# Masking the second attention's scores on TensorE, and handing its subtraction from GpSimd to VectorE

## What is computed

```python
q = (Q @ Wq_w + Wq_b).reshape(b, tq, H, DK).transpose(0, 2, 1, 3)      # 16 heads of 16
k = (K @ Wk_w + Wk_b).reshape(b, tk, H, DK).transpose(0, 2, 1, 3)      # 64 keys a batch
scores = jnp.einsum('bhqd,bhkd->bhqk', q, k) / jnp.sqrt(jnp.float32(DK))
scores = jnp.where(mask == 0, jnp.float32(-1000000000.0), scores)      # one mask of 512 x 64
attn = jax.nn.softmax(scores, axis=-1)
out = jnp.einsum('bhqk,bhkd->bhqd', attn, v)
x = x + jnp.tanh(g_xattn[1]) * (out @ Wo_w + Wo_b)
```

## Time and profile before

| | before |
|---|---|
| median of 3 runs | 811.75 us (811.11 to 812.29) |
| the profiled execution | 812.6 us, span 811.1 us |
| mean granted TensorE clock | 0.925 |
| busy in the span: PE, DVE, ACT, POOL | 82%, 63%, 41%, 28% |
| second attention's ticks, first `bounded` to the last tile's `bounded` | from 444.57 to 549.35 us |

### The profile page before, as it was taken

How to read it: one execution, slowest core, us unless ns; L and a number is a source line. 1 busy time by engine, 2 the same in 40 slices (tenths; PEclk the granted TensorE clock), 3 DMA queues, 4 the chain that set the end, 5 groups by cost and what they waited for, 6 DMA issues and landing times. The chain is left out here.

```text
span 811.1 us, 15016 instructions
## 1 busy us (share of the span) xinstructions
PE 666.6 (82%) x4947; PEld 613.2 (76%) x4948; DVE 510.2 (63%) x1271; ACT 328.9 (41%) x554; POOL 226.7 (28%) x336
## 2 busy tenths in 40 slices
PE   3798943898999889999734668686997889999995
PEld 3566633898999889998733446466997889999995
DVE  6844553788544786445577687794665775565556
ACT  7544313556333554334363354326432523343331
POOL 7532342000000000000064666367001711011152
PEclk9999855999999999999967789989998999999998
DMA  7999217544300359500040001000004411111124
GB/s 279 418 417 400 81 42 258 186 145 183 109 26 26 126 165 304 194 26 26 19 131 26 26 1 53 0 1 1 1 1 143 183 47 43 36 52 52 34 72 141
DMA packets 22997, 90.70 MB, mean 112 GB/s; under 512 B 4402, under 2 KB 8755, under 8 KB 17363
## 3 DMA queue, kind: packets, MB, share of 16 engines
q1 hardware_dynamic: 15794, 68.64, 22.9%
q0 software_dynamic: 7168, 21.63, 8.9%
HBM read 50.94 MB, written 45.61 MB: 119 GB/s over the span
## 5 line engine op out<-in xcount | busy, mean ns | idle before, releaser
L1559 ACT ACTIVATE e_h<-psum,e_be 128x256 f32<-128x256 f32 x144 | 67.6, 474 | 142.6 <-PE psum L52 140.1
L50 PE MATMUL psum<-e_h_hi,e_w_hi 128*128 128x256 f32 x384 | 110.3, 287 | 6.2 <-DVE e_w_lo L1631 5.5
L51 PE MATMUL psum<-e_h_lo,e_w_hi 128*128 128x256 f32 x384 | 107.9, 281 | 0.0
L52 PE MATMUL psum<-e_h_hi,e_w_lo 128*128 128x256 f32 x384 | 107.8, 281 | 0.0
L1623 DVE CAST e_h_hi<-e_h 128x256 fp32r<-128x256 f32 x144 | 43.5, 302 | 83.2 <-ACT e_h L1559 83.2
L1894 ACT ACTIVATE vz<-psum,fb 128x256 f32<-128x256 f32 x112 | 52.5, 475 | 99.9 <-PE psum L52 99.7
L50 PEld LDWEIGHTS psum<-e_h_hi,e_w_hi 128*128 128x128 f32 x384 | 72.3, 188 | 9.7 <-DVE e_w_lo L1631 8.8
L52 PEld LDWEIGHTS psum<-e_h_hi,e_w_lo 128*128 128x128 f32 x384 | 72.4, 188 | 0.0
L51 PEld LDWEIGHTS psum<-e_h_lo,e_w_hi 128*128 128x128 f32 x384 | 72.4, 188 | 0.0
L1625 DVE TENSOR_TENSOR e_h_lo<-e_h,e_h_hi 128x256 fp32r<-128x256 f32 x144 | 61.3, 425 | 4.9
L50 PE MATMUL psum<-e_gT_hi,e_w_hi 128*128 128x256 f32 x192 | 55.8, 291 | 9.5 <-DVE e_w_lo L1698 7.8
(11 more groups left out here) (415 smaller groups left out, 2144.2 us busy)
## 6 DMA issues: line engine op xcount, KB each, us to landing
xs<-zeros SPq DMA_DIRECT2D x18, 1024.0 KB, 17.6
e_w_raw<-in_W SPq DMA_DIRECT2D x18, 1024.0 KB, 5.2
ys<-zeros SPq DMA_DIRECT2D x6, 1024.0 KB, 24.1
ys<-e_yo POOLq DMA_DIRECT2D x14, 256.0 KB, 3.5
e_xg<-xs POOLq DMA_DIRECT2D x13, 256.0 KB, 6.5
e_w_raw<-in_W SPq DMA_DIRECT2D x6, 512.0 KB, 8.0
f_w_lo<-fw SPq DMA_DIRECT2D x6, 512.0 KB, 7.0
ys<-x_norm POOLq DMA_DIRECT2D x10, 256.0 KB, 2.5
```

The lines of the kernel that those rows point to most:

```text
L50: nc.tensor.matmul(out, wh, xh, start=start, stop=False)
L51: nc.tensor.matmul(out, wh, xl, start=False, stop=False)
L52: return nc.tensor.matmul(out, wl, xh, start=False, stop=stop)
L1559: nc.scalar.activation(h32[:, m % RING], ps[:, HIDDEN_BANKS[m % RING], 0:SLOT], ACT.Gelu, bias=be[:, m:m + 1]).then_inc(gelu_ok, 1)
```

## The change

A mask value is no longer applied by DVE as it reads the banks. `off` holds 0 or -2^100 for each row and key, in the form TensorE takes, and a fourth matmul for each bank (the identity times `off`, repeated for the 8 heads) adds it to the scores in PSUM. DVE then takes the maxima straight from the banks, and subtracts them from the banks again into `s_sc`; GpSimd's subtraction is gone. In its place GpSimd adds the two halves of each head's 64 exponentials into a tile `pairs` (16 x 32), which DVE sums. `scores(n+1)` waits for the end of DVE's subtraction, where it waited for the end of the clamping.

```diff
@@ gpsimd
             for n in range(NT + 1):
-                if n < NT:
-                    pool.wait_ge(mx_ok, n + 1)
-                    nc.gpsimd.tensor_tensor(sc[:, n % 3], sc[:, n % 3], top[:, n % 2, :, None].to_broadcast([P, HEADS, KEYS]),
-                                            ALU.subtract).then_inc(sub_ok, 1)
-                if 1 <= n < NT + 1:
+                if n:
+
+                    pool.wait_ge(p_ok, n)
+                    if n >= 2:
+                        pool.wait_ge(den_ok, n - 1)
+                    p = sc[:, (n - 1) % 3]
+                    nc.gpsimd.tensor_tensor(pairs[:], p[:, :, 0:KEYS // 2], p[:, :, KEYS // 2:KEYS], ALU.add).then_inc(add_ok, 1)
                     pool.wait_ge(sum_ok, n)
@@ vector
-            def bounded(n):
+            def differences(n):
+
                 dve.wait_ge(s_done, n + 1)
+                masked = ps[:, 6:8, :].rearrange("p c (h n) -> p (c h) n", h=HPC)
+                nc.vector.tensor_reduce(top[:, n % 2], masked, AX.X, ALU.max).then_inc(mx_ok, 1)
+                dve.wait_ge(mx_ok, n + 1)
                 if n >= 3:
                     dve.wait_ge(pt_done, n - 2)
-                nc.vector.scalar_tensor_tensor(out=sc[:, n % 3], in0=ps[:, 6:8, :].rearrange("p c (h n) -> p (c h) n", h=HPC), scalar=MASKED,
-                                               in1=cap[:, n % TB, None, :].to_broadcast([P, HEADS, KEYS]),
-                                               op0=ALU.max, op1=ALU.min).then_inc(cl_ok, 1)
-                dve.wait_ge(cl_ok, n + 1)
-                if n >= 2:
-                    dve.wait_ge(sub_ok, n - 1)
-                nc.vector.tensor_reduce(top[:, n % 2], sc[:, n % 3], AX.X, ALU.max).then_inc(mx_ok, 1)
+                nc.vector.tensor_tensor(sc[:, n % 3], masked, top[:, n % 2, :, None].to_broadcast([P, HEADS, KEYS]),
+                                        ALU.subtract).then_inc(sub_ok, 1)
 
             def reciprocals(n):
-                dve.wait_ge(p_ok, n + 1)
+                dve.wait_ge(add_ok, n + 1)
                 if n >= 2:
                     dve.wait_ge(nm_ok, n - 1)
-                nc.vector.tensor_reduce(den[:, n % 2], sc[:, n % 3], AX.X, ALU.add).then_inc(den_ok, 1)
+                nc.vector.tensor_reduce(den[:, n % 2], pairs[:], AX.X, ALU.add).then_inc(den_ok, 1)
@@ vector, constants
-            nc.vector.tensor_scalar(cap[:], mask_i[:], 0.0, HUGE - MASKED, ALU.not_equal, ALU.mult).then_inc(cap_ok, 1)
-            dve.wait_ge(cap_ok, 1)
-            nc.vector.tensor_scalar(cap[:], cap[:], MASKED, None, ALU.add).then_inc(cap_ok, 1)
+            nc.vector.tensor_copy(ident_r[:], k["ident"][:]).then_inc(off_ok, 1)
+            nc.vector.tensor_scalar(off[:], mask_i[:], 0.0, HIDE, ALU.is_equal, ALU.mult).then_inc(off_ok, 1)
@@ tensor
                 if n:
-                    pe.wait_ge(cl_ok, n)
+                    pe.wait_ge(sub_ok, n)
                 t = slice(i * P, (i + 1) * P)
                 for c in range(C):
-                    last = mm3(nc, ps[:, 6 + c, :], qT_hi[:, b % 2, c, t], qT_lo[:, b % 2, c, t],
-                               kz_hi[:, b, c, :], kz_lo[:, b, c, :], True, True)
+                    mm3(nc, ps[:, 6 + c, :], qT_hi[:, b % 2, c, t], qT_lo[:, b % 2, c, t],
+                        kz_hi[:, b, c, :], kz_lo[:, b, c, :], True, False)
+                    last = nc.tensor.matmul(ps[:, 6 + c, :].rearrange("p (h n) -> p h n", n=KEYS), ident_r[:],
+                                            off[:, i, None, :].to_broadcast([P, HPC, KEYS]), start=False, stop=True)
                 last.then_inc(s_done, 1)
```

More of the change, by code:

```diff
@@ L33 @@
 EPS = 1e-5
-MASKED = -1e9 * HD ** 0.5
 SCALE = HD ** -0.5
-HUGE = 3e38
+HIDE = -float(2 ** 100)
 RSQRT_SEED = 0x5F3759DF
@@ L711, in softmax_attention @@
         rw, rw_hi, rw_lo = sb("rw", [P, C, E1]), sb("rw_hi", [P, C, E1], F32R), sb("rw_lo", [P, C, E1], F32R)
-        mask_i, cap = sb("mask_i", [P, TB, KEYS], I32), sb("cap", [P, TB, KEYS])
+        mask_i, one = sb("mask_i", [P, TB, KEYS], I32), sb("one", [P, KEYS])
+        off, ident_r = sb("off", [P, TB, KEYS], F32R), sb("ident_r", [P, P], F32R)
+        pairs = sb("pairs", [P, HEADS, KEYS // 2])
         sc = sb("sc", [P, 3, HEADS, KEYS])
@@ L719, in softmax_attention @@
         uh_hi, uh_lo = (t[:].rearrange("p a c s -> p (a c s)").rearrange("p (m n) -> p m n", n=SLOT) for t in (qT_hi, qT_lo))
-        c_ld, cst_ok, cap_ok, bo0 = sem("c_ld"), sem("cst_ok"), sem("cap_ok"), sem("bo0")
+        c_ld, cst_ok, off_ok, bo0 = sem("c_ld"), sem("cst_ok"), sem("off_ok"), sem("bo0")
         wh_ok, wl_ok = sem("wh_ok"), sem("wl_ok")
@@ L728, in softmax_attention @@
         q_done, qh_ok, ql_ok = sem("q_done"), sem("qh_ok"), sem("ql_ok")
-        s_done, cl_ok, mx_ok, sub_ok, p_ok, den_ok, sum_ok, nm_ok = (
-            sem(n) for n in ("s_done", "cl_ok", "mx_ok", "sub_ok", "p_ok", "den_ok", "sum_ok", "nm_ok"))
+        s_done, mx_ok, sub_ok, p_ok, add_ok, den_ok, sum_ok, nm_ok = (
+            sem(n) for n in ("s_done", "mx_ok", "sub_ok", "p_ok", "add_ok", "den_ok", "sum_ok", "nm_ok"))
         pt_done, pc_ok, pv_done, oh_ok, ol_ok = (sem(n) for n in ("pt_done", "pc_ok", "pv_done", "oh_ok", "ol_ok"))
@@ L1029, in _ @@
             nc.vector.tensor_copy(bo_hi[:], bo[:]).then_inc(cst_ok, 1)
-            nc.vector.memset(cap[:, 0, :], 1.0).then_inc(cst_ok, 1)
+            nc.vector.memset(one[:], 1.0).then_inc(cst_ok, 1)
             dve.wait_ge(cst_ok, 3)
@@ L1033, in _ @@
             nc.vector.tensor_tensor(bo_lo[:], bo[:], f32(bo_hi[:]), ALU.subtract).then_inc(cst_ok, 1)
-            nc.vector.tensor_copy(ones_r[:].rearrange("p (a n) -> p a n", a=2), cap[:, 0:1, :].to_broadcast([P, 2, KEYS])).then_inc(cst_ok, 1)
-            dve.wait_ge(cst_ok, 6)
-            nc.vector.tensor_scalar(cap[:], mask_i[:], 0.0, HUGE - MASKED, ALU.not_equal, ALU.mult).then_inc(cap_ok, 1)
-            dve.wait_ge(cap_ok, 1)
-            nc.vector.tensor_scalar(cap[:], cap[:], MASKED, None, ALU.add).then_inc(cap_ok, 1)
+            nc.vector.tensor_copy(ones_r[:].rearrange("p (a n) -> p a n", a=2), one[:, None, :].to_broadcast([P, 2, KEYS])).then_inc(cst_ok, 1)
+            nc.vector.tensor_copy(ident_r[:], k["ident"][:]).then_inc(off_ok, 1)
+            nc.vector.tensor_scalar(off[:], mask_i[:], 0.0, HIDE, ALU.is_equal, ALU.mult).then_inc(off_ok, 1)
             norm_1(0)
@@ L1054, in _ @@
             norm_1(2)
-            dve.wait_ge(cap_ok, 2)
             for n in range(TICKS):
@@ L1058, in _ @@
                 if n < NT:
-                    bounded(n)
+                    differences(n)
                 if 1 <= n < NT + 1:
@@ L1178, in first_layer @@
                     if q < 2:
-                        pe.wait_ge(cl_ok, NT)
+                        pe.wait_ge(sub_ok, NT)
                     else:
@@ L1223, in _ @@
             pe.wait_ge(cst_ok, 6)
+            pe.wait_ge(off_ok, 2)
             pe.wait_ge(kzh_ok, HPC)
```

## The result

The changed kernel is slower: 827.24 us against 811.43 us for the kernel before on the same chip, a ratio of 1.0204 (95% interval 1.0174 to 1.0234). The profiled execution took 826.65 us, span 825.2 us, mean granted TensorE clock 0.923. The prediction was 825.3 us, 818.5 to 830.5.

The account below looks back on a forecast made before the run. The ticks were taken as bounded by waits between engines, mostly a chain of DVE, PE's scores, ACT's queue and DVE's sum. Nine terms summed to 13.6 us on the median 811.75, giving 825.3 us, range 818.5 to 830.5.

Parts of the forecast that it names:

- Banks free: Before the scores: banks held through maxima and then subtraction, so PE starts 1.25 us later wherever it waits for them.
- the items: The prediction's nine numbered terms along the chain of ticks 0 to 16, from -0.5 to +2.7 us, together 13.6 us.
- Two more matmuls: PE's scores: two more matmuls of 512 columns cost 0.47 us at full clock, 0.85 at half clock.
- Halving sum: GpSimd ahead of DVE's sum: 1.25 less 0.54, 0.7 us longer through exponential and sum; 0.54 shorter in DVE's queue alone.
- Item 3: Tick 4, where DVE's queue (a layer norm) sets the time: 0.5 us shorter.
- Behind 557.70 the shift is carried by a full PE: After tile 14's multiplication: GpSimd's last work at most 2 us later, hidden under PE work, so the shift stays 13.6 us.
- Item 8: Ticks 12 and 13: +0.7 us, GpSimd's long subtraction now standing before a sum that DVE waits for.
- DVE sets the period, and the time falls: Rival: the ticks' chain is DVE's queue, each of 16 ticks 0.54 us shorter, 803.1 us; 7 in 100.
- The milder one: Rival: the low end, around 820.5 us, as PE with more work in the scores may keep its clock; 25 in 100.
- The heavier one: Rival: around 829 us, from slow halving sums, half clock everywhere or a dearer PSUM read; 16 in 100.
- the 0.065 us: DVE's maxima: the skill page's estimate of a PSUM read's extra time over SBUF; the prediction left it out of its sum.

Follow-up runs that it names:

- pe_waits_max: Kernel before, with PE's scores waiting for the end of the maxima instead of the clamping: stretch 123.6 us, 8.9 more; ratio 1.0107.
- full_sum: Changed kernel without GpSimd's halving sum, DVE summing all 64 exponentials of a head: stretch 125.6 us, 7.6 less than the changed kernel; ratio 1.0110.
- exp_first: Kernel before, with ACT's exponential of the last tile only moved ahead of `q_hi` and the attention's high-half copy: stretch 111.5 us; ratio 0.9982.
- exp_early: Kernel before, exponential ahead of `q_hi` in ACT's queue and, every fourth tick, ahead of the transposes' copy: stretch 111.2 us, 3.6 less; ratio 0.9953.
- no_mask_mm: Changed kernel without the 32 matmuls that add the mask, so no mask is applied: stretch 132.3 us, 0.9 less; ratio 1.0171.
- late_w1: Changed kernel with GpSimd's second long weight subtraction moved from tick 15 to 16: stretch 131.0 us, 2.2 less; ratio 1.0198.
- extra_mm: Kernel before with the 32 mask matmuls added and DVE's clamping kept: stretch 120.1 us, 5.4 more; ratio 1.0051.
- halve_before: Kernel before with GpSimd's halving sum added behind its subtraction, DVE summing 32 instead of 64: stretch 143.3 us, 28.6 more; ratio 1.0349.
- after_early: Changed kernel with ACT's queue reordered as in exp_early: stretch 121.2 us; ratio 1.0075 to the kernel before.
- full_early: Changed kernel without its halving sum and with ACT's queue reordered as in exp_early: stretch 115.14 us; ratio 1.0023 to the kernel before.

## Why the prediction was right, and where it was not

**What held.** Sign, mechanism and size: 13.6 us forecast up to the multiplication of tile 14, 14.4 measured, and a median 2 us above the forecast one. The signs that it named came out: maxima and subtraction at 1.22, the halving sum at 1.27 (1.2 forecast), DVE's sum at 0.68, 116.3 us from the first to the last tile's reading (112 to 116 forecast). PE's wait for the banks rose to 19.7 us, just short of the "over 20" forecast. From `project(2)` to the first scatter of the routing it took 67.8 us instead of 67.2, so that part kept its length.

**Banks free (1.25 a pass).** Right in mechanism, shown alone by pe_waits_max: +8.9 us, where the items hold some 6.7 for it. The other 2.2 us go with the lower clock (0.79 instead of 0.86), which the items left to the matmuls' term; no run takes the two apart.

**Two more matmuls.** This term was mis-sized. The items hold some 3.6 us for it; the runs gave 0.9 (taken out of the changed kernel) and 5.4 (added to the one before). If the hold of the banks costs the changed kernel what it cost the one before, it is 2 us dearer than its items, and the matmuls, at 0.9, are 2.7 us cheaper: two errors of opposite sign, which the total hides. So the 0.8 us at the multiplication of tile 14 is in part luck.

**Halving sum.** 3.4 us in the items up to tile 14, 3.6 by full_sum. Item 3 was -1.1 instead of -0.5: the DVE instruction that reads two operands in SBUF took 1.74 us before (from 475.29 on, beside the end of GpSimd's subtraction, with GpSimd's multiplication from 475.90 on, itself slowed to 2.88 us), and 1.19 after. Timelines of the profile before and of the profile after:

```profile
475.29 1.74 DVE L948 SCALAR_TENSOR_TENSOR x_res<-x_norm,tg,x_res 128x1024 f32<-128x1024 f32 x1
```

```profile
474.04 1.91 POOL L810 TENSOR_TENSOR s_sc<-s_sc,s_top 128x1024 f32<-128x1024 f32 x1 [3.13 <-DVE s_top L978]
475.90 2.88 POOL L814 TENSOR_TENSOR s_sc<-s_sc,s_rden 128x1024 f32<-128x1024 f32 x1
```

```profile
474.39 1.19 DVE L951 SCALAR_TENSOR_TENSOR x_res<-x_norm,tg,x_res 128x1024 f32<-128x1024 f32 x1
474.56 2.79 POOL L817 TENSOR_TENSOR s_sc<-s_sc,s_rden 128x1024 f32<-128x1024 f32 x1 [2.28 <-DVE s_rden L988]
```

The Trainium skill, page "GPSIMD Engine Reference", section "Specifications", says that GpSimd and VectorE share their way to SBUF and get in one another's way when VectorE has two inputs there; the slowed pair of before agrees. After, only GpSimd's side of the pair is slowed. In these rows it is each time the instruction that started second that is longer: DVE's, 1.25 us into the subtraction, then GpSimd's multiplication behind it; after, GpSimd's, 0.17 us behind DVE's. Two places are too few for a rule.

**The step that failed** is "Behind 557.70 the shift is carried by a full PE: the last multiplication and the weights' subtractions on GpSimd come later by 2 us more at most, under several us of PE work". PE was not yet full: `project(2)` waits for an `xT_lo` that stands in DVE's queue behind the last sum, and that sum now waits for GpSimd. Item 8 had found this very link behind tick 12; behind tick 15 I followed the multiplication and not DVE's queue. It cost 4.0 us, shown from two sides: gone without the halving sum, and 2.2 us smaller with the long subtraction moved. That the median is off by only 2 us although this is missing is in part luck: the profiled execution of the changed kernel started the stretch 2.8 us early. On the second chip the change cost 17.4 us of the median (817.62 to 835.0), nearer to the stretch's 18.4 than to the 13.6 forecast.

**The rivals.** *DVE sets the period, and the time falls* is dead: with ACT's queue reordered, where DVE would have its best chance, the change without its halving sum is still 4.0 us longer in the stretch than the reordered kernel before. (Its eight matmuls at full clock are 2.0 us by the figures it gives, not 2.1; nothing hangs on that.) *The milder one* failed at its premise: the clock did fall (0.86 to 0.84 over the first 111 us, and to 0.81 with fewer matmuls). *The heavier one* came near in time on the second chip (1.0226 x 811.43 = 829.8) but not by its reasons: the halving sum took 1.27 us, maxima and subtraction 1.22, and the clock over the stretch was 0.82, not 0.5. That ACT's queue behind PE is on the chain is shown by exp_first and exp_early, which shorten the stretch by 3.3 and 3.6 us. That is far from the 9 expected, since two thirds of what DVE no longer waits for the exponentials (11.0 us) it then waits for PE and for ACT's other work.

**What stays open.** What decides which ticks PE runs at 1.2 GHz. The runs show that the outcome repeats for one kernel (two profiles each of the two kernels, the stretch within 0.1 us) and flips between near kernels, not a rule by which I could have worked it out. The parts' own prices (8.9, 5.4, 7.6) are given by single edits in kernels that differ in clock and in GpSimd's queue, and are not a partition of the 18.4. No run has the banks' hold taken out of the changed kernel. Why whole executions of one kernel differ by some 6 us behind the routing was not tried.

## What to carry to other kernels

When work moves from an idle engine to the one that holds a shared buffer, count the time that the buffer stays held, not the busy time: DVE and GpSimd did 15 us less in this stretch, and it became 18 us longer. When a step is put in another engine's queue, read for every place what stands ahead of it there and what stands behind its waiter, up to the point where an engine is truly full; the one place not read so cost 4 us, and the halving sum behind a subtraction cost 28.6. Where PE idles between short groups of matmuls, as in this stretch, the price of 32 of them was good to a few us only (0.9 and 5.4): compare the granted clock of each stretch before believing in a gain or a loss.

## What the runs showed of the hardware

Less work on PE went with a lower clock and gained only 0.9 us (no_mask_mm, 0.81 against 0.84), and the 2.2 us of a stretch that ended earlier were given back within 18 us of full work at clock 0.79 instead of 0.91 (late_w1). In the 60 us behind `project(2)` the kernels fall in two groups: a clock of 0.95 to 0.96 (both kernels, full_sum, no_mask_mm, extra_mm, pe_waits_max, exp_early), and one of 0.89 to 0.90 (late_w1, halve_before, exp_first, after_early, full_early), worth 2.5 to 4 us up to the routing. VectorE's maxima over 1024 fp32 numbers took the same from PSUM as from SBUF (1.218 and 1.220 us), with none of the 0.065 us that the prediction quoted. GpSimd's sum of two 512-wide inputs took 1.27 us, over half of the 2.35 to 2.39 of a 1024-wide operation on two.
